# Mamba scan: four of sixteen state inputs made by matmuls with a scaled identity, and an h*C ring of six

## The reference

```python
x = silu(conv4(x)); x_dbl = x @ x_proj_w.T
dt = softplus(x_dbl[..., :8] @ dt_proj_w.T + dt_proj_b)
Bm, Cm = x_dbl[..., 8:24], x_dbl[..., 24:]
dA  = exp(dt[..., None] * A)                    # A = -exp(A_log), 256 channels x 16 states
dBx = (dt * x)[..., None] * Bm[:, :, None, :]
h = dA_t * h + dBx_t                            # over the tokens
y = einsum('bdn,bn->bd', h, C_t)                # then + x * D, * silu(z), @ out_proj_w.T
```

## Time and profile before

| | us |
|---|---|
| median of 3 runs | 2819.32 (2819.3 to 2819.78) |
| the profiled execution, own time | 2823.07 |
| its span, first to last instruction | 2821.0 |
| PE busy in the span | 2458.8 (87%) |
| DVE busy | 2216.2 (79%) |
| ACT busy | 1698.4 (60%) |
| POOL busy | 1432.5 (51%) |

### The profile page before, as it was taken

How to read it: one execution, slowest core, us unless ns; L and a number is a source line. 1 busy time by engine, 2 the same in 40 slices (tenths; PEclk the granted TensorE clock), 3 DMA queues, 4 the chain that set the end, 5 groups by cost and what they waited for, 6 DMA issues and landing times. The chain is left out here.

```text
span 2821.0 us, 35553 instructions
## 1 busy us (share of the span) xinstructions
PE 2458.8 (87%) x10516; PEld 1557.5 (55%) x10516; DVE 2216.2 (79%) x4289; ACT 1698.4 (60%) x2971; POOL 1432.5 (51%) x1482
## 2 busy tenths in 40 slices
PE   6998487878889888877799499979999999997999
PEld 5776243333334434324677388855555555546887
DVE  7998489989999999998899555458877777755444
ACT  3676566557656666643578365536776767764555
POOL 2474698888888988884277450033232323310000
PEclk8999698999999999999899799979999999998999
DMA  2256222222222222222157310000000000001000
GB/s 76 62 163 117 84 75 71 73 68 75 68 72 75 75 76 72 75 77 67 28 136 146 97 40 1 0 16 1 1 1 1 2 1 1 1 1 42 8 8 15
DMA packets 99496, 146.05 MB, mean 52 GB/s; under 512 B 13036, under 2 KB 50540, under 8 KB 99124
## 3 DMA queue, kind: packets, MB, share of 16 engines
q1 hardware_dynamic: 82196, 98.60, 11.5%
q0 software_dynamic: 16608, 44.78, 7.3%
q10 hardware_dynamic: 512, 0.53, 0.1%
HBM read 124.98 MB, written 18.87 MB: 51 GB/s over the span
## 5 line engine op out<-in xcount | busy, mean ns | idle before, releaser
L1756 POOL TENSOR_TENSOR a_hc<-a_H,a_cb 128x512 f32<-128x512 f32 x512 | 620.3, 1233 | 134.7 <-DVE a_H L1619 127.1
L1411 PE MATMUL a_Y<-a_hc,ident 128*128 128x512 f32 x1024 | 543.7, 642 | 57.9 <-POOL a_hc L1756 49.8
L2112 ACT ACTIVATE a_pt<-a_W 128x512 f32<-128x512 f32 (+3 forms) x768 | 346.2, 496 | 202.1 <-PE a_W L2012 198.3
L1537 ACT ACTIVATE a_dA<-a_dt,a_aneg 128x512 f32<-128x512 f32 x512 | 342.8, 715 | 191.7 <-POOL a_dt L1775 100.2
L1411 PEld LDWEIGHTS a_Y<-a_hc,ident 128*128 128x128 f32 x1024 | 185.7, 198 | 312.0 <-POOL a_hc L1756 216.5
L1643 DVE TENSOR_TENSOR a_BX<-a_u,a_BX 128x1024 f32<-128x1024 f32 x256 | 308.7, 1211 | 35.7 <-PE a_BX L1345 24.9
L1619 DVE TENSOR_TENSOR_SCAN a_H<-a_dA,a_H,a_BX 128x512 f32<-128x512 f32 x256 | 312.4, 1263 | 3.6 <-ACT a_dA L1537 3.6
L2335 POOL TENSOR_SCALAR_AFFINE_SELECT a_pt<-a_pt 128x512 f32<-128x512 f32 x128 | 91.1, 712 | 422.8 <-ACT a_pt L2112 422.8
L1619 DVE TENSOR_TENSOR_SCAN a_H<-a_dA,a_BX 128x512 f32<-128x512 f32 x256 | 296.7, 1203 | 0.9 <-POOL a_hc L1756 0.9
L2198 DVE CUSTOM_DVE_ANT_0 a_masked<-a_W,a_mask 128x384 f32<-128x384 f32 (+3 forms) x512 | 231.8, 487 | 80.5 <-PE a_W L1999 78.4
L2012 PE MATMUL a_W<-a_Q,a_K 128*128 128x512 f32 (+3 forms) x768 | 283.6, 385 | 1.7 <-ACT a_pt L2112 1.6
(11 more groups left out here) (323 smaller groups left out, 5444.6 us busy)
## 6 DMA issues: line engine op xcount, KB each, us to landing
a_cb<-a_crow SPq DMA_DIRECT2D x256, 256.0 KB, 3.2
m_orows<-m_yt SPq DMA_DIRECT2D x46, 256.0 KB, 2.5
t_wst<-ternary_w SPq DMA_DIRECT2D x22, 256.0 KB, 2.7
m_xrows<-m_xn SPq DMA_DIRECT2D x16, 256.0 KB, 2.3
m_xg<-m_xrows,m_gidx POOLq DMA_INDIRECT x184
out<-x SPq DMA_DIRECT2D x8, 256.0 KB, 2.3
m_wg<-moe_ws SPq DMA_DIRECT2D x2, 516.0 KB, 4.5
a_hc<-mamba_conv_rows SPq DMA_DIRECT2D x1, 1024.0 KB, 5.1
```

The lines of the kernel that those rows point to most:

```text
L1411: pe.matmul(Y[:, h, :], ident[:], hc[:, g % HCRING, :], start=False, stop=v == NS - 1).then_inc(s_y, 1)
L1537: act.activation(dA[:, G % ARING, :], dt[:, b % 2, h, :], ACT.Exp, scale=aneg[:, d, h, v:v + 1]).then_inc(s_dA, 1)
L1756: pool.tensor_tensor(hc[:, G % HCRING, :], H[:, s, span], cb[:, v % RING, :], ALU.mult).then_inc(s_hc, 1)
L2112: act.activation(pt[:, u % PR, 0:BLK - r * P], W[:, 3 + u % 3, 0:BLK - r * P], ACT.Exp).then_inc(s_exp, 1)
```

## The change

For states 8, 10, 12 and 14 of every block but the first, the product u times B is no longer made by VectorE. In `by_diagonal`, TensorE makes it directly in both PSUM banks: for each half and each 128 tokens, a matmul of the transposed u (stationary) with a 128x128 diagonal matrix that holds B's values of that state and those tokens. ScalarE makes the four diagonals of a state (`diagonal`) by scaling the identity with B's column, into `wi`, one buffer that the next state needs again. For that, u and B are transposed on TensorE through O ("uT", "bT" in `uses_of`) and copied by ScalarE: uT of the first half in slot 14 of the block before, of the second half in slot 2 or 1, bT in slot 4 or 3. For those states the B row, `rows`, is left out. VectorE waits for TensorE's result (`s_tx`) ahead of the scans of such a state, and ahead of the product of the state after it. The ring `hc` shrinks from eight halves to six.

```diff
-    HCRING = 8
+    HCRING = 6
...
+    BY_PE = (8, 10, 12, 14)
+    def on_pe(Q):
+        return Q >= NS and Q % NS in BY_PE
+    def made_by(pe, Q):
+        return sum(on_pe(q) == pe for q in range(Q + 1))
...
+        if has_scan(b):
+            uses.update({2 if t < 2 else 1: ("uT", 1, b), 4 if t < 2 else 3: ("bT", 0, b)})
+        if b + 1 < NB:
+            uses[14] = ("uT", 0, b + 1)
...
# TensorE
                     Q = b * NS + v
-                    if Q >= NB * NS:
+                    if Q >= NB * NS or on_pe(Q):
                         return
...
+                def by_diagonal(b, v):
+                    Q = b * NS + v
+                    if not on_pe(Q):
+                        return
+                    pe.wait_ge(s_dg, made_by(True, Q))
+                    pe.wait_ge(s_Oa, through("A", b, 4))
+                    pe.wait_ge(s_scan, 2 * Q - 3)
+                    for h in range(HALF):
+                        out = BX[:, row_bank(Q) if h else half_bank(Q), :]
+                        for t in range(TPB):
+                            at = slice(t * P, (t + 1) * P)
+                            mm = pe.matmul(out[:, at], uT[:, h, at], wi[:, at], start=True, stop=True)
+                    mm.then_inc(s_tx, 1)
...
+                    elif kind == "uT":
+                        pe.wait_ge(s_u, 2 * tb + part + 1)
+                        for t in range(TPB):
+                            at = slice(t * P, (t + 1) * P)
+                            mm = pe.transpose(O[:, at], u[:, tb % 2, part, at], ident[:])
+                    elif kind == "bT":
+                        pe.wait_ge(s_dbl, tb + 1)
+                        for t in range(TPB):
+                            mm = pe.transpose(O[:, t * NS:(t + 1) * NS], dbl[0:NS, tb % 2, t * P:(t + 1) * P],
+                                              ident[0:NS, 0:NS])
...
                         if v in uses:
                             o_use(b, v, uses[v])
+                        if has_scan(b) and v + 1 < NS:
+                            by_diagonal(b, v + 1)
                         if has_scan(b) and v:
                             add_y(b, v - 1)
...
# ScalarE
+                    elif kind == "uT":
+                        act.activation(uT[:, part, :], O[:], ACT.Copy).then_inc(s_Oa, 1)
+                    elif kind == "bT":
+                        act.activation(bT, O[:, 0:TPB * NS], ACT.Copy).then_inc(s_Oa, 1)
...
+                def diagonal(b, v):
+                    Q = b * NS + v
+                    if not on_pe(Q):
+                        return
+                    act.wait_ge(s_Oa, through("A", b, 4))
+                    wait(act, s_tx, made_by(True, Q) - 1)
+                    for t in range(TPB):
+                        last = act.activation(wi[:, t * P:(t + 1) * P], ident[:], ACT.Copy,
+                                              scale=bT[:, t * NS + v:t * NS + v + 1])
+                    last.then_inc(s_dg, 1)
...
                             decay(b, v + LEAD)
+                            if v + 2 < NS:
+                                diagonal(b, v + 2)
...
# VectorE
-                    dve.wait_ge(s_bx, G + 1)
+                    if on_pe(G // 2):
+                        dve.wait_ge(s_tx, made_by(True, G // 2))
+                    else:
+                        dve.wait_ge(s_bx, 2 * made_by(False, G // 2))
...
+                            if not on_pe(Q):
+                                dve.wait_ge(s_B, made_by(False, Q))
+                                if Q and on_pe(Q - 1):
+                                    dve.wait_ge(s_tx, made_by(True, Q - 1))
+                                wait(dve, s_scan, 2 * Q - 3)
+                                dve.tensor_tensor(both_banks(Q), u[:, b % 2, :, :],
+                                                  BX[:, row_bank(Q), :].unsqueeze(1).broadcast_to([P, HALF, BLK]),
+                                                  ALU.mult).then_inc(s_bx, 2)
```

More of the change, by code:

```diff
@@ L1175, in uses_of @@
                     10: ("z", 0, 0), 11: ("z", 1, 0),
-                    13: ("xp", 0, 2)}
+                    13: ("xp", 0, 2), 14: ("uT", 0, 1)}
         t = b % 4
@@ L1202, in silus_of @@
         return {9: (b + 2, None)} if b + 2 < NB else {}
-    COUNTED = {"O": ("T", "x", "z", "xp", "dt", "out"), "D": ("T", "out"), "A": ("x", "z", "xp", "dt")}
+    COUNTED = {"O": ("T", "x", "z", "xp", "dt", "out", "uT", "bT"), "D": ("T", "out"),
+               "A": ("x", "z", "xp", "dt", "uT", "bT")}
     ORDER = [(b, v, u[0]) for b in range(-1, NB + 1) for v, u in sorted(uses_of(b).items())]
@@ L1243, in mamba @@
         cb = sb("cb", [P, RING, BLK])
+        uT = sb("uT", [P, HALF, BLK])
         ab, ee, ln, uu = (sb(n, [P, BLK]) for n in ("ab", "ee", "ln", "uu"))
@@ L1270, in mamba @@
         s_B = sem("B")
+        s_dg, s_tx = sem("dg"), sem("tx")
         s_cb = [sem(f"cb{r}") for r in range(RING)]
@@ L1282, in mamba @@
                  (wo[:], w["out_proj"]))
+        bT = alog[:].rearrange("p e h n -> p (e h n)")
         sels = dA[0:DBC, 0:RING, :].rearrange("p a (n c) -> p (a n) c", c=P)
@@ L1343, in rows @@
                     if Q % NS == 2:
-                        pe.wait_ge(s_bx, 2 * Q - 2)
+                        pe.wait_ge(s_bx, 2 * made_by(False, Q - 2))
                     pe.matmul(BX[:, row_bank(Q), :], sel[:, Q % NS, :], bcs[:, Q // NS % 4, :], start=True, stop=True)\
                       .then_inc(s_B, 1)
+                def by_diagonal(b, v):
[11 more added lines that the diff above has]
+                    mm.then_inc(s_tx, 1)
                 def o_use(b, v, use):
@@ L1410, in add_y @@
                         pe.wait_ge(s_hc, b * UB + g + 1)
-                        pe.matmul(Y[:, h, :], ident[:], hc[:, g % HCRING, :],
+                        pe.matmul(Y[:, h, :], ident[:], hc[:, (b * UB + g) % HCRING, :],
                                   start=False, stop=v == NS - 1).then_inc(s_y, 1)
@@ L1640, in _ @@
                                 dve.wait_ge(s_u, 2 * (b + 1))
-                            dve.wait_ge(s_B, Q + 1)
-                            wait(dve, s_scan, 2 * Q - 3)
-                            dve.tensor_tensor(both_banks(Q), u[:, b % 2, :, :],
-                                              BX[:, row_bank(Q), :].unsqueeze(1).broadcast_to([P, HALF, BLK]),
-                                              ALU.mult).then_inc(s_bx, 2)
+                            if not on_pe(Q):
[6 more added lines that the diff above has]
+                                                  ALU.mult).then_inc(s_bx, 2)
                             if v:
```

## The result

| kernel | median us (lowest to highest) | ratio to before, 95% interval |
|---|---|---|
| before, same runs | 2819.55 (2819.3 to 2822.9, 4 runs) | |
| changed | 2864.94 (2859.83 to 2869.97, 4 runs) | 1.0157 [1.0135, 1.0178] |

The change makes the kernel 45 us slower, 1.6%. The sign and the mechanism of the forecast (2839) held, and its range (2813 to 2866) by 1 us; its size, 20 us, did not.

What follows compares the result with a forecast made beforehand. VectorE, busy 918 of the Mamba stage's 961 us, was taken as the bound. Against 67.2 us saved stood 91.65 of waits and 4 for transposes, less 8 of slack: + 20 us, 2839 us, range 2813 to 2866.

Steps and rivals of the forecast that it cites:

- The waits at the products of 9, 11, 13 and 15: VectorE waits for states made on TensorE before these products, 91.65 us over all blocks.
- dt ahead of state 8: On TensorE, a dt projection of 0.86 us precedes state 8 in three of four kinds of block.
- ScalarE's diagonal ahead of state 12: State 12's diagonal queues behind silus, softplus and decays: waits of 3.6, 3.3, 3.8 us in three block kinds.
- the convolution ahead of state 8: x convolutions in slots 5 and 6 leave TensorE behind: waits of 3.75 us in block 10, 2.55 in block 11.
- The ring costs nothing: Cutting the h*C ring to six adds no time; GpSimd's wait for Y was 6.5 us with eight.
- 0.3 in 13 blocks makes 4: Added transposes on TensorE in slots 1 to 4 cost VectorE 4 us, with ends of 0 and 13.
- The 0.6 that the forecast put on state 8: In block 8, added transposes make TensorE some 0.6 us late, within a wait of 1.8 at the product of 9.
- 60 x 1.12 = 67 us: VectorE time saved by removing four products of 1.12 us in each of fifteen blocks.
- taken as 8: VectorE pauses let GpSimd and TensorE catch up, giving back 8 us of idle time, between 0 and 20.
- TensorE keeps up: Rival: TensorE's lag shrinks when VectorE pauses, waits stay near 0.3 us each, 2770 us; chance 0.15.
- ScalarE isn't late: Rival: state 12 comes as TensorE allows, some 2 us earlier, 2819 us, no change; chance 0.12.
- The clock falls ahead of state 12: Rival: ten blocks run state 12's matmuls at 1.2 GHz, 1.95 us more each, 2858 us; chance 0.13.

Runs made afterwards that it cites:

- experiment 2: Changed kernel with TensorE's matmuls of state v+1 put ahead of the slot's use of O: 2881.1 us, ratio 1.0213 to the kernel before.
- experiment 3: Changed kernel with ScalarE making one diagonal a block, state 8's, used for all four states (results left wrong): 2844.11 us, ratio 1.0080 to the kernel before.
- experiment 5: Changed kernel with two diagonal buffers, ScalarE scaling earlier, and an h*C ring of five: 2847.49 us, ratio 1.0091 to the kernel before.
- experiment 7: Changed kernel with two diagonal buffers, states ahead of O's use, and second-half convolution and dt later in blocks with b % 4 of 2 and 3: 2840.58 us.
- experiment 4: Kernel before with only the h*C ring cut to six: 2820.47 us, ratio 0.9998 to the kernel before.
- experiment 1: Changed kernel with no state made on TensorE; transposes, copies and ring of six kept: 2833.85 us, ratio 1.0048 to the kernel before.
- experiment 8: Changed kernel timed again, nothing altered: 2865.32 us, ratio 1.0148 to the kernel before.
- experiment 10: Changed kernel with no state on TensorE and u's transposes moved to slots 8 or 9 and 11 or 12: 2835.66 us, ratio 1.0042 to the kernel before.
- experiment 9: Changed kernel with only state 10 made on TensorE, preparation kept: 2830.51 us, ratio 1.0040 to the kernel before.
- experiment 11: Changed kernel with u's transposes late and only state 14 on TensorE, ahead of O's use: 2834.14 us, ratio 1.0042 to the kernel before.

## Why the prediction was right, and where its size was wrong

*Right.* The waits at the products of 9, 11, 13 and 15, 91.65 us in the forecast, are 89.9. In block 8 they are 1.25, 0.32, 3.46 and 0.97 against 1.8, 0.3, 3.6 and 1.65 (ahead of the last, an add to x of 0.66 covers part), in block 10 4.40 and 3.80 for the two long ones against 3.75 and 3.8. Experiments 2, 3 and 5 show the causes given: dt ahead of state 8, ScalarE's diagonal ahead of state 12; experiment 7 shows the third, the convolution ahead of state 8. TensorE waits for the diagonal of 12 in nine blocks, by 1.0 to 1.7 us (forecast ten, 2). The ring costs nothing (experiment 4).

*Luck.* That the sum comes within 2 us is partly luck, since single blocks miss by more, both ways: blocks 1 and 3 wait 8.3 and 9.1 us (forecast 5.0 and 6.85), block 2 and block 4 5.6 and 5.8 (8.15 and 7.35). In blocks 1, 4 and 5 the matmuls of one state each took 3.62 to 3.65 us, TensorE's lower level, which was in no term of the sum. And the range held by 1 us only because of its two extras, a slow clock ahead of state 12 in ten blocks and 8 us for the added wait instructions; the first came in one block, and no run shows the second by itself.

*The steps that failed* are three other terms of the sum, all mis-sized towards a better time, in the profiled execution by 18.7 us together:

- "0.3 in 13 blocks makes 4", the transposes. Alone they cost 13 us (experiment 1). The forecast priced them by the time that TensorE works on them and left out what they wait for: O, which has to be read first. TensorE stands idle for 29.5 us ahead of them in experiment 1, and 8.3 of the 12.0 us by which the B-row waits grew lie in the four blocks with b % 4 = 2, which have such stops, none in those with 1, which have the same transposes without a stop in slots 1 to 4. The 0.6 that the forecast put on state 8 in block 8 for the same work did not come (1.25 for 1.8). In the changed kernel itself 9.6 us of longer B-row waits are left, 5.6 above the forecast; 5.8 of them are the four waits of 1.46 at the product of 4 in blocks 2, 6, 10 and 14.
- "60 x 1.12 = 67 us", the saving. It was 59.0. 1.12 us is a product's share of a stream in which one instruction starts 0.09 us before the last one ends (874.44 + 2.33 is 0.09 past 876.68). A VectorE that waits loses that overlap, and its product takes 1.23 us instead of 1.21: 0.11 for each of 60 waits, 6.6 us. The adds of L122 took 1.8 more. 67.2 - 8.4 = 58.8.
- "taken as 8", the slack given back. "Issue" gave 4.9 and other idle time took 1.8, so 3.

20.4 + 5.6 + 8.2 + 4.9, less 1.7 for the state waits, is 37.4, what the profiled executions show. The medians lie 8.6 further apart, since the profile of before was 3.5 above its median and the one after 5.1 below; the two profiles of the changed kernel (experiment 8) differ mostly in the waits for TensorE.

One reading was off without touching the sum: by the earlier trace rows GpSimd and TensorE stand 10 and 12% behind VectorE (824 and 806 of 918 us), not 12 and 16%.

*The rivals.* "TensorE keeps up" fell, for the reason given against it, and for a wider one: part of what is taken off one wait comes back at another (experiments 2 and 7), TensorE being busy in 877 of 1003 us. "ScalarE isn't late" fell with experiment 3. "The clock falls ahead of state 12" fell as well: from 810 us on the granted clock of the changed kernel is 1.00 of 2.4 GHz (before 0.98), and after 1.70 us without a matmul the state took 2.05 us. It was near, though: in experiment 2 the gap is 3.7 us, and the clock does fall (3.43 us). The Trainium skill (TensorE: Matmul & The Clock Gate, Part 1: The HAM clock gate) has the slow level as the default that activity lifts; the rows of experiment 2 agree, and those of the changed kernel show slow matmuls behind one of its nine shorter waits ahead of state 12.

*What stays open.* That the stop at O is what makes the preparation dear is read from the traces of experiments 1 and 10; no run took the stop away and kept the transposes (B's later, or a bank of their own), so how much of the 13 us would go is not shown. Nor is it shown why one state, moved alone, gains only 1.5 to 3.3 us (experiments 9 and 11).

## What to carry to other kernels

Where a second engine stands 12% behind the bound, work moved from the one to the other gains only the difference of what it saves and of the waits that it sets up; here 1.1 us of VectorE were bought with 1.8 us of TensorE (less a B row), and a well-placed state gained at most 1.5 to 3.3 us in all, hardly clear of the scatter, against 12 or 13 for the preparation. Price added work on an in-order engine not by its own time alone: ask which buffer it needs, who has to read that buffer first, and what stands behind it in the queue meanwhile. And where two in-order engines feed each other, moving an operation forward on one delays what the other has behind it (experiment 2).

## What the runs showed of the hardware

- VectorE starts an instruction 0.09 us before the last one ends, but not after a wait that holds it; a change that sets up a wait for each instruction it removes loses a tenth of the saving. The Trainium skill (VectorE: DVE Perf Modes, The DRAIN you can't avoid) says that a semaphore after each of a row of copies costs nothing extra. For a semaphore that is already there when VectorE comes the rows agree (the overlap of the earlier trace rows stands across such waits); for one that holds it they show 0.11 us beyond the wait itself.
- TensorE, busy by its records for 83 to 84% of the stage beside VectorE's 94% (experiments 1 and 10), already delayed VectorE: the B-row waits grew by 12 to 13 us, and part of the rest of TensorE's time was no slack, since it stood idle for 25.7 to 29.5 us ahead of the transposes until O had been read. The Trainium skill (Perfetto Trace Analysis, Identifying the Most-Contended Engine) says that a matmul's busy share is not a good measure of how close a kernel is to roofline; no run here tests its reason, the pipelining.
- Transposes of 128x128 float32 are recorded once each, not twice as the float32 matmuls are, and four keep TensorE's queue for 0.44 to 0.47 us, as long as the earlier trace rows gave for four of the 16 records (1.79 / 4 = 0.45).
- Behind the nine gaps of 1.0 to 1.7 us that ScalarE's diagonal left in the changed kernel, the matmuls of state 12 took 2.05 us eight times and 3.65 once (at 666 us; the granted clock was 0.95 from 500 to 700 us); behind those of 3.67 us and more in experiment 2 they took 2.47 to 3.78 every time. In between it goes both ways: behind stops of 1.80 to 1.93 us four Y matmuls took 1.98 us in six of six blocks of the changed kernel, and 3.08 and 3.68 us in two of three of experiment 10.
